# Row statistics of the second batch made between score sums, and one accumulator scaled inside a group, in a gated attention and sign-weight FFN block

## What is computed

```python
x = x + tanh(g_xattn[0]) * xattn(layernorm(x), k_cache=ctx, v_cache=ctx, wq, wk, wv, wo)
x = x + tanh(g_ffn[0])   * ffn(layernorm(x), sign(up_w), sign(down_w), up_scale, down_scale, output_scale)
# xattn: q, k_new, v_new = x wq^T, x wk^T, x wv^T;  k = [ctx, k_new], v = [ctx, v_new]
#        softmax(q k^T / sqrt(512)) v  wo^T
# ffn:   relu((x sign(up_w)^T) * up_scale) sign(down_w)^T * down_scale * output_scale
```

## Time and profile before

| what | value |
|---|---|
| median of 3 runs | 601.21 us (600.84 to 603.96) |
| the profiled execution, its own time | 599.61 us |
| its span | 597.8 us |
| granted TensorE clock, mean | 0.998 of full speed |
| PE busy | 587.9 us (98%), 2738 matmuls |
| DVE busy | 380.9 us (64%) |
| ACT busy | 289.9 us (48%) |
| POOL busy | 118.8 us (20%) |
| chain that ended last | PE 93%, DVE 3%, DMA 2%, ACT 1% |

### The profile page before, as it was taken

How to read it: one execution, slowest core, us unless ns; L and a number is a source line. 1 busy time by engine, 2 the same in 40 slices (tenths; PEclk the granted TensorE clock), 3 DMA queues, 4 the chain that set the end, 5 groups by cost and what they waited for, 6 DMA issues and landing times.

```text
span 597.8 us, 7100 instructions
## 1 busy us (share of the span) xinstructions
PE 587.9 (98%) x2738; PEld 486.5 (81%) x2738; DVE 380.9 (64%) x532; ACT 289.9 (48%) x426; POOL 118.8 (20%) x111
## 2 busy tenths in 40 slices
PE   8999999899999999999999999999999999999997
PEld 6888888788888888888888888888887878888885
DVE  4697717788454587454587786755459734766654
ACT  3784401574321464321566565655659444645531
POOL 4006300403003002003011016232322002242002
PEclk9999999999999999999999999999999999999999
DMA  8614014032010153020112223120111301230011
GB/s 298 213 71 138 5 31 139 7 105 72 1 72 0 18 194 106 1 71 1 71 42 85 87 70 106 35 72 35 59 49 35 136 11 66 72 141 36 0 71 70
DMA packets 20097, 43.21 MB, mean 72 GB/s; under 512 B 4832, under 2 KB 4832, under 8 KB 19680
## 3 DMA queue, kind: packets, MB, share of 16 engines
q1 hardware_dynamic: 20064, 42.76, 20.9%
HBM read 36.45 MB, written 6.30 MB: 72 GB/s over the span
## 4 chain that ended last, share of the span: by engine, by line
PE 93%; DVE 3%; DMA 2%; ACT 1%; SPq 0%; issue 0%; ACTq 0%
PE proj L540 34%; PE score L670 19%; PE turn L655 12%; PE score L573 9%; PE score L540 5%; PE proj L655 5%; PE proj L573 4%; PE turn L532 2%; PE score L804 2%; DMA rows<-in_x 1%; DMA raw_ctx<-in_ctx_turned 1%; PE turn L638 1%; PE proj L638 1%; DVE four_x L1190 0%; DVE four_x L1323 0%; DVE turned_x L1318 0%
## 5 line engine op out<-in xcount | busy, mean ns | idle before, releaser
L670 PE MATMUL score<-down_signs,hid_split 128*128 128x512 f32 x512 | 133.8, 390 | 0.6 <-DVE normed L1552 0.5
L670 PEld LDWEIGHTS score<-down_signs,hid_split 128*128 128x128 f32 x512 | 95.8, 188 | 21.7 <-DVE hid_split L1519 0.9
L540 PE MATMUL proj<-probsT,four_x 128*128 128x512 f32 x384 | 89.3, 391 | 0.0
L540 PEld LDWEIGHTS proj<-probsT,four_x 128*128 128x128 f32 x384 | 71.5, 188 | 14.6
L540 PE MATMUL proj<-four_x,weights 128*128 128x512 f32 x336 | 77.2, 390 | 1.6 <-ACT raw_new L899 1.6
L540 PEld LDWEIGHTS proj<-four_x,weights 128*128 128x128 f32 x336 | 62.9, 188 | 15.1 <-ACT raw_new L899 2.0
L465 POOL TENSOR_TENSOR four_x<-raw_ctx,four_x 128x2048 fp32r<-128x2048 f32 x7 | 32.6, 4655 | 192.6 <-ACT four_x L885 192.6
L1519 DVE TENSOR_TENSOR hid_split<-hid,hid_split 128x512 fp32r<-128x512 f32 x64 | 44.0, 690 | 15.8 <-ACT hid_split L1109 15.6
L893 ACT ACTIVATE four_x<-proj 128x512 fp32r<-128x512 f32 x32 | 19.1, 597 | 67.6 <-PE proj L540 67.6
L540 PE MATMUL proj<-weights,four_x 128*128 128x512 f32 x192 | 51.9, 405 | 0.0
L655 PE MATMUL turn<-ops_b,up_ops 128*128 128x512 f32 x192 | 51.8, 391 | 0.0
(11 more groups left out here) (128 smaller groups left out, 871.3 us busy)
## 6 DMA issues: line engine op xcount, KB each, us to landing
raw_w<-in_ffn_w SPq DMA_DIRECT2D x24, 512.0 KB, 3.3
raw_ctx<-in_ctx_turned SPq DMA_DIRECT2D x4, 1024.0 KB, 5.3
raw_ctx<-in_ctx SPq DMA_DIRECT2D x4, 1024.0 KB, 5.8
result<-rows SPq DMA_DIRECT2D x16, 256.0 KB, 2.0
rows<-in_x SPq DMA_DIRECT2D x3, 1024.0 KB, 7.5
turned_x<-in_x_turned SPq DMA_DIRECT2D x3, 1024.0 KB, 5.3
rows_away<-rows SPq DMA_DIRECT2D x1, 2048.0 KB, 14.5
rows<-rows_away SPq DMA_DIRECT2D x1, 2048.0 KB, 7.8
```

Source lines behind the costliest of these rows:

```text
L540: last = pe.matmul(bank, lhs(l), rhs(r), start=start and i == 0, stop=stop and i == 2)
L670: last = pe.matmul(wide(r), hid_split[:, n % HR, s, r * P:(r + 1) * P], down_signs[:, chunk_of(q), :], start=(q == 0 and s == HI), stop=(q ...
```

## The change

Batch 1's statistics are split up: on DVE three of the four row tiles come between the score sums of batch 0, the fourth and the moments and means between the low parts of its turned probabilities. On POOL `inverse_std(1)` comes ahead of the four low parts of W_O. In batch 0, `norm_turned(1)` comes behind attention output e == 1 and `next_rows_low(1)` behind e == 2, on ACT too. In the FFN `scale_even(1, 0)` moves from behind the sums of group 8 to a place inside them.

```diff
@@ POOL @@
                 if b == 0:
+                    inverse_std(1)
                     for i in range(DC):
                         weight_low(W_O, i)
-                    inverse_std(1)
@@ ACT @@
-                    if e == (3 if b == 0 else 1):
+                    if e == (2 if b == 0 else 1):
                         act.wait_ge(turned_normed, b + 1)
                         act.activation(xT[:, HI], turned_x[:, :, :], ACT.Copy).then_inc(next_hi, 1)
@@ DVE, batch @@
                 queries(b)
+                if b == 0:
+
+                    dve.wait_ge(x_in[1], 16)
+                    norm_stats(RT, 1)
                 sum_scores(b, AT_C22, 0)
+                if b == 0:
+                    norm_stats(RT + 1, 1)
                 sum_scores(b, AT_C22, 1)
+                if b == 0:
+                    norm_stats(RT + 2, 1)
                 sum_scores(b, AT_C21, 0)
...
                 probs_out(b, 1)
+                if b == 0:
+                    norm_stats(RT + 3, 1)
                 probs_out(b, 2)
+                if b == 0:
+                    norm_moments(1)
                 proj_out(b, 1, chunk(new_side, 1))
                 probs_out(b, 3)
+                if b == 0:
+                    means(1)
...
                 probs_out(b, 7)
-                if b == 0:
-                    dve.wait_ge(x_in[1], 16)
-                    norm_stats(RT)
-                    norm_moments(1)
-                    means(1)
...
-                        if e == (3 if b == 0 else 0):
+
+                        if e == (1 if b == 0 else 0):
                             norm_turned(b + 1)
-                        if e == (3 if b == 0 else 1):
+                        if e == (2 if b == 0 else 1):
                             next_rows_low(b + 1)
@@ DVE, sums_of_products @@
                 hidden_low(2 * pair, 2 * j)
                 if g == 0:
                     attend(BATCH - 1, 0)
+                if g == HG:
+                    scale_even(1, 0)
@@ DVE, FFN @@
             sums_of_products(1, 0)
-            scale_even(1, 0)
             scale_even(1, 2)
```

More of the change, by code:

```diff
@@ L1520, in hidden_low, with scale_even @@
                                   ALU.subtract).then_inc(hid_ready, 1)
+            def scale_even(c, r):
+                dve.wait_ge(down_done, RT * (HC * c + HC - 1) + r + 1)
+                dve.tensor_tensor(scaled(c, r), wide(r), out_gain[:, :], ALU.mult).then_inc(acc_scaled, 1)
             def sums_of_products(pair, j):
@@ L1548, in sums_of_products @@
                 hidden_low(2 * pair, 2 * j + 1)
-            def scale_even(c, r):
-                dve.wait_ge(down_done, RT * (HC * c + HC - 1) + r + 1)
-                dve.tensor_tensor(scaled(c, r), wide(r), out_gain[:, :], ALU.mult).then_inc(acc_scaled, 1)
             def scale_odd(c, r):
```

## The result

| what | before | after |
|---|---|---|
| median of 9 runs | 601.06 us (599.94 to 603.96) | 597.24 us (596.69 to 599.5) |
| ratio, 95% interval | | 0.9949, 0.9933 to 0.9965 |
| the profiled execution, its own time | 599.61 us | 597.95 us |
| its span | 597.8 us | 596.2 us |

The account below looks back on a forecast made before the run. PE, busy for 98% of the span, was taken as the bound, so only its waits could be gained: 601.21 - 1.93 (attention) - 0.2 (FFN) = 599.1 us. Range 597.8 to 601.5 us; within 0.5%: 0.80.

Parts of the forecast that it names:

- The first wait: PE's wait at a key job of batch 1 for ACT's copy L899 would vanish, gaining 1.93 us.
- the difference of two equal stretches: Attention outputs to next scores: 56.37 us for batch 0, 54.44 for batch 1, so batch 0 loses 1.93 us.
- a start at 89.6: DVE's norm_turned could start as late as 89.6, 1.8 us earlier than before, and PE's wait for L899 would be gone.
- The cover of the statistics: Batch 1's statistics, 0.62 us each, fit DVE's idle gaps between score sums and low parts, costing 0.
- so 1.9 us are free there: Slack at PE's first turn of probabilities, 52.95 to 54.89, to cover score sums that slip; 1.9 us.
- The second wait: PE's FFN wait for DVE's scaling moves from group 9's first down piece to its second and shrinks, gaining 0.2 us.
- the step from ACT's copy to PE: Group 9's second down piece starts no earlier than 0.15 us after ACT's first copy ends: 492.85 against 493.11, 0.26 gained.
- The restart: PE restarting behind a down piece in group 9 would take some 0.06 us off the 0.26 gained.
- The sum: Whole kernel: 1.93 and 0.2 us off, 2.13 in all, from the median 601.21 to 599.1 us.
- A: FFN: ACT is not held up and PE's wait for the scaling goes whole, 0.81 us; 598.5 us, chance 0.12.
- B: Attention: PE's wait for L899 stays under another name, only the scaling's gain is left; 601.0 us, chance 0.10.
- C: Batch 0's scores: statistics held up beside POOL, PE stands for 4.4 us; 603.5 us, chance 0.06.

Follow-up runs that it names:

- e1: Changed kernel with the FFN scaling put back behind group 8, so the attention part alone; 597.63 us beside 599.43 before, ratio 0.9961.
- e5: Changed kernel with norm_turned and next_rows_low of batch 0 each one attention output later; inner time (first score product to last addition) 557.55 us.
- e3: Changed kernel with norm_turned and next_rows_low of batch 0 back behind the fourth attention output, statistics still early; inner time (first score product to last addition) 559.47 us.
- e6: Changed kernel with all four statistics of batch 1 in one piece behind the first half's sum C21; inner time (first score product to last addition) 559.07 us.
- e7: Changed kernel with ACT's two copies of block 1's odd accumulators ahead of the next up weights' sign in group 8; 596.90 us beside 599.65 before, ratio 0.9956.
- e2: Kernel before with only the scaling moved inside group 8; 598.91 us beside 599.43, ratio 0.9991.
- e8: The changed kernel again without any edit, against the kernel before; 597.36 us beside 599.65, ratio 0.9963.
- e9: e7's kernel with 16 instead of 8 filler matmuls at the start; 596.65 us, ratio to the kernel before 0.9944.

## Why the prediction was right, and where not

*The first wait.* Right in place and size: 1.93 us forecast, 1.93 in the stretch, 1.95 in e1. Reading it as the difference of two equal stretches was worth it: the idle time of 1.62 us alone would have missed 0.3. The statement that a start at 89.6 is early enough fits e5 (85.61, no wait) and e3 (91.11, the whole wait), but no run came closer to it. The store took 1 us longer than the quickest of before, inside 10.6 to 16.7.

*The cover of the statistics.* Right: the sums start within 0.1 us of where they did, and a statistic takes 0.68 us as a single row, or 0.62 as one of four, beside POOL too. What was wrong here is the slack that I named in case the cover failed: "so 1.9 us are free there". That is the slack of the first turn alone. e6 shows that a link two turns further on is tighter: DVE's low part of the first turned probabilities ended at 57.9 and PE's third turn began at 58.6. DVE's and PE's timelines, kernel before:

```profile
57.22 0.68 DVE L1190 TENSOR_TENSOR probsT<-turn,probsT 128x512 fp32r<-128x512 f32 x1
```

```profile
58.56 0.60 PE L532 MATMUL turn<-ident,probs 128*128 128x128 f32 x4
```

In the real change nothing slipped, so this cost the forecast nothing; it would have misled anyone who put more in.

*The second wait.* Right in mechanism, link by link: DVE's sum C21 0.47 late, ACT's list moved as a whole, the wait handed from the first `down` piece to the second. Forecast 0.2, measured 0.30. The term was mis-sized in the step from ACT's copy to PE: I let the `down` piece start 0.59 + 0.15 = 0.74 us after the copy's start at the earliest, and in the changed kernel it started 0.63 after it (490.70 and 491.33). So the piece came about 0.4 us earlier than before, not 0.26. The restart went the other way: it cost 0.11 us (the next product came 0.57 us after the piece, where it is 0.46 without a wait), and I had taken off 0.06.

*The sum.* 2.13 us forecast, 2.21 in the inner time. The median of 597.24 lies 0.6 us below my range (597.8 to 601.5), and the change of 0.51% just outside the half per cent to which I gave four in five. The weak step is the last, from the profiled execution to a median: I took 601.21 for fixed and allowed 0.6 us around it, while medians of the kernel before ranged from 601.06 down to 599.43, comparison by comparison. The profiled execution, 599.61, lay below all nine of the first comparison and at the medians of the later ones. Carried over by the ratio to the 601.21 that the range was built on, the result is 598.1 us, inside the range. The ratios are the firmer measure, and both intervals hold 0.9963. That the first one came out at 0.9949 was not foreseen, and where its last 0.14% comes from stays open.

*Rivals.* A didn't come with this change, but e7 shows that its full 0.81 us was there to be had, with one more edit. B didn't come: PE has no wait for L899, and the facts were there before DVE asked for them. C is out by e6: the mechanism that it needed, statistics held up by POOL, didn't show, even with all four right beside POOL's pass. Its place was well chosen though, since e6 lost 1.49 us right there once the cover was gone.

## What to carry to other kernels

Work that is moved into an engine's idle gaps must fit gap by gap: statistics of 0.62 to 0.68 us in gaps of 0.67 cost nothing, the same four in a piece cost 1.49 us, though the list as a whole had room. A chain over several engines is shortened only if both its data and its place on the in-order lists come early: here each half alone gave nothing or a loss. When an instruction goes ahead of another on a full list, look up who waits for the one that is pushed back, and reorder that engine's list too: e7's two lines gave more than the scaling's move itself.

## What the runs showed of the hardware

*The clock falls in the start of some executions.* The three profiled executions with the latest first score product (e2, e6, e8: 36.0 to 36.3 us, against 34.0 to 35.0 in the others) show a granted clock of about 0.5, the 1.2 GHz level, between 12 and 14 us. The stretch from 12 to 14 us of e8 (us, PE, PEld, DVE, ACT, POOL busy, then granted clock, DMA share, GB/s):

```profile
12.00:14.00 2.00, 2.00 (x12) 2.00 (x11) 1.15 (x3) 0.00 (x0) 1.11 (x2) 0.50 1.03 389
```

and of e7:

```profile
12.00:14.00 2.00, 2.00 (x19) 2.00 (x18) 1.10 (x3) 0.00 (x0) 1.16 (x2) 1.00 1.03 390
```

PE had stood idle between the fillers and the first key products for 1.5 us in each of the three, and for 0.3 to 1.6 us in the others; then it ran 12 matmuls in two microseconds in the one and 19 in the other. The idle time alone doesn't decide: the longest of all, 1.58 us, is the changed kernel's, and its clock stayed at 1.00.

The timed runs fit a cost. In e9's comparison the three executions of the kernel before with a mean clock of 0.997 took 601.2 to 602.2 us, and the five with 0.999 or 1.000 took 598.7 to 599.6. But a mean clock is a weak sign of it. It has another part at the end, where PE has no work left. The last full microsecond of the kernel before (mean clock 0.998), whose clock had not fallen in the start:

```profile
596.00:597.00 1.00, 0.00 (x0) 0.00 (x0) 0.00 (x0) 0.00 (x0) 0.00 (x0) 0.51 0.97 365
```

Only the three profiled executions with the slow start have a mean below 0.998 (0.996 and 0.997). Nor is this all of the scatter, since an execution of 601.3 us in e1's comparison has a mean clock of 1.0. A different share of slow starts on both sides could make up the first ratio's 0.14% beyond the traces. That isn't shown: the clocks of the kernel before aren't on record for that comparison, and only one execution of each kernel is profiled.

*DVE beside POOL.* The statistics (one SBUF input) weren't slowed beside POOL's pass in e6. But two other instructions were: the sum of keys with two SBUF inputs, 4.69 us in the earlier trace rows and 1.22 alone, and, in e5, a copy of four elements per partition that takes 0.17 us in the changed kernel, away from the pass:

```profile
104.27 2.23 DVE L1329 COPY mean_rstd<-mean_var 128x4 f32<-128x4 f32 x1
```

```profile
101.86 4.61 POOL L465 TENSOR_TENSOR four_x<-raw_ctx,four_x 128x2048 fp32r<-128x2048 f32 x1 [27.46 <-ACT four_x L885]
```

The copy ends at 106.50, when POOL's pass ends at 106.47. This agrees with the Trainium skill (SBUF — State Buffer, SBUF: two separate sides), by which DVE in a two-port mode, or with two SBUF inputs against a POOL instruction that reads SBUF, and POOL take the shared ports in turn and for a whole instruction. In which mode the copy ran, the trace doesn't say. In both rows the price is about what was left of POOL's instruction, 2.2 us for the copy and 3.6 us for the sum of keys, whatever the size of DVE's.
